# One scatter pass of a four-layer graph network: the attribute loads move to ScalarE's queue, a turn multiplies its own unit, and its sums are added in the last three steps

## The reference, cut to what matters

```python
def _gin_conv(x, src, dst, W_a, b_a, W_b, b_b):
    agg = jax.ops.segment_sum(x[src], dst, num_segments=N)
    h = agg + x
    ...
# in the spline layer, used much later:
v = edge_attr * (KS - 1)            # edge_attr: 3 numbers an edge
lo = jnp.floor(v); f = v - lo
...
basis = jnp.prod(w, axis=-1)        # weights of the 8 corners of a 4x4x4 grid cell
```

## Time and profile before

| | us |
|---|---|
| median of 3 runs | 14964.41 |
| the runs | 14935.78 to 14974.39 |
| span of the profiled execution | 14974.7 |
| TensorE's mean granted clock, share of full speed | 0.750 |
| start of the first basis of turn 0 (DVE) | 69.56 |
| start of the first basis of turn 12 (DVE) | 1876.23 |
| first product of the node phase behind the pass (PE) | 2054.82 |

### The profile page before, as it was taken

How to read it: one execution, slowest core, us unless ns; L and a number is a source line. 1 busy time by engine, 2 the same in 40 slices (tenths; PEclk the granted TensorE clock), 3 DMA queues, 4 the chain that set the end, 5 groups by cost and what they waited for, 6 DMA issues and landing times.

```text
span 14974.7 us, 218620 instructions
## 1 busy us (share of the span) xinstructions
PE 8996.9 (60%) x45542; PEld 5742.7 (38%) x45542; DVE 7299.2 (49%) x21322; ACT 1842.2 (12%) x1480; POOL 10378.6 (69%) x10674
## 2 busy tenths in 40 slices
PE   4655569986665665777776767776777760023225
PEld 2322223333443443444544444444445440023214
DVE  5555532323223224666666666666666661244446
ACT  4444420000000000111111111111111110000000
POOL 6666627775776775777775777775777765777772
PEclk7677669998787887777777877777777775566667
DMA  5666645554776774111111111111111111122221
GB/s 169 215 218 215 218 131 181 176 179 137 257 259 212 256 255 133 22 22 22 22 22 22 22 23 22 22 22 21 23 23 22 23 19 34 36 50 52 46 45 44
DMA packets 1184028, 1456.97 MB, mean 97 GB/s; under 512 B 415010, under 2 KB 627140, under 8 KB 1183173
## 3 DMA queue, kind: packets, MB, share of 16 engines
q10 hardware_dynamic: 565552, 1132.67, 21.6%
q0 software_dynamic: 338944, 197.81, 8.1%
q1 hardware_dynamic: 278678, 119.14, 3.5%
HBM read 1129.74 MB, written 319.05 MB: 97 GB/s over the span
## 4 chain that ended last, share of the span: by engine, by line
POOL 52%; issue 22%; PE 10%; DVE 6%; DMA 4%; DVEq 3%; ACT 1%; SPq 0%; POOLq 0%; ACTq 0%
POOL work L740 52%; PE ps L933 3%; PE ps L919 2%; PE ps L839 1%; DMA work<-tab_sp,idx 1%; DMA idx<-in_src_tile 1%; ACT nodes L1211 1%; PE ps L854 1%; DMA work<-in_x,idx 1%; DVE big L1709 1%; DVE work L1778 1%; DVEq L1635 1%; DVE work L1789 0%; PE ps L1036 0%; PE ps L953 0%
## 5 line engine op out<-in xcount | busy, mean ns | idle before, releaser
L740 POOL DMA_INDIRECT work<-tab_sp,idx x4992 | 4725.9, 947 | 1790.6 <-issue 1775.4
L933 PE MATMUL ps<-work 128*128 128x192 f32 x9984 | 2855.9, 418 | 1759.1 <-DVE work L1789 1035.7
L933 PEld LDWEIGHTS ps<-work 128*128 128x128 f32 x9984 | 1922.3, 229 | 2571.6 <-DVE work L1789 2244.1
L1789 DVE TENSOR_TENSOR work<-work,ps 128x192 f32 x4992 | 1762.6, 353 | 1628.8 <-PE ps L933 1101.0
L740 POOL DMA_INDIRECT work<-tab_att,idx x1664 | 1766.3, 1061 | 657.9 <-issue 507.0
L740 POOL DMA_INDIRECT work<-tab_gcn,idx x1664 | 1590.5, 956 | 556.5 <-issue 549.5
L854 PE MATMUL ps<-nodes,work 128*96 128x384 bf16 (+1 forms) x6664 | 1731.0, 381 | 174.5 <-DMA nodes<-counts_d 111.1
L919 PE MATMUL ps<-work,wk 128*32 128x144 f32 x10080 | 1780.3, 330 | 7.4 <-DVE work L1789 6.8
L740 POOL DMA_INDIRECT work<-in_x,idx x1248 | 1247.0, 999 | 702.5 <-issue 383.2
L1645 DVE TENSOR_TENSOR big<-big,ps 32x12 f32 (+2 forms) x3936 | 619.6, 157 | 2094.2 <-PE ps L827 1163.8
L1248 ACT ACTIVATE work<-zero 128x2496 f32<-128x2496 f32 x318 | 725.4, 2282 | 5489.0 <-PE ps L919 5482.9
(11 more groups left out here) (225 smaller groups left out, 5615.2 us busy)
## 6 DMA issues: line engine op xcount, KB each, us to landing
nodes<-counts_d ACTq DMA_DIRECT2D x468, 1056.0 KB
counts_d<-nodes ACTq DMA_DIRECT2D x104, 2376.0 KB
nodes<-counts_d ACTq DMA_DIRECT2D x144, 1320.0 KB
work<-counts_d ACTq DMA_DIRECT2D x117, 1056.0 KB
work<-tab_sp,idx POOLq DMA_INDIRECT x4992
work<-basis_d SPq DMA_DIRECT2D x312, 160.0 KB
work<-edge_rows SPq DMA_DIRECT2D x112, 320.0 KB
edge_rows<-work ACTq DMA_DIRECT2D x104, 320.0 KB, 2.4
```

Source lines behind the costliest of these rows:

```text
L740: pool.indirect_dma_start(out=rows(p, r)[:, t, 0:ROW[p]], out_offset=None, in_=TABLE[p], in_offset=bass.IndirectOffsetOnAxis(ap=idx[:, r, ...
L933: nc.tensor.matmul(ps[:, t % SUB, 0:K12 * TW], u0[:, s % 2, t % SUB, :], vb[:, t % SUB, :, :].rearrange("p k j -> p (k j)"), start=True, s ...
L1789: v.tensor_tensor(to, to, got, ALU.add).then_inc(mom_added.sem, 1)
```

## The change

SP keeps only the index loads. ACT asks for the attributes of steps 0 and 1 ahead of the pass, and for those of step k + 2 in step k. In ACT's queue the wait for the basis, and its write, move from ahead of the first eviction to behind the fifth. Turn i multiplies unit i instead of i - 1: two chunks in each of the first four steps, behind the third and the sixth tile of counts, and one in the fifth (turn 0, whose own counts must be written first, does three in each of its last three steps). The pieces are asked for behind the fourth and the seventh eviction of a step, the first two of a turn at the end of the turn before. DVE adds oct 0 in the sixth step of a turn, oct 1 in the seventh, octs 2 and 3 in the eighth (turn 0 adds all four at its end). Nothing is left to multiply after turn 12. The twelve register values of a step's near sums are read in one load instead of three of four.

```diff
+        def gin1_chunk(o, x, first):
+            c = 3 * (o - (STEPS - 3)) + x if first else 2 * o + x if x < 2 else NCH
+            return c if 0 <= c < NCH else None
+        def gin1_loads(o, b, first):
+            place = {(o, 3): [2 * o + 2], (o, 6): [2 * o + 3]}
+            if first:
+                place = {(4, 3): [0, 1], (5, 3): [2], (5, 6): [3], (6, 0): [4], (6, 3): [5], (6, 6): [6], (7, 0): [7],
+                         (7, 3): [8]}
+            return [c for c in place.get((o, b), []) if c < NCH]
...
 # SP, index_loads("gin1")
-                    def turn_(i, ahead):
-                        for o in range(STEPS):
-                            k, h = STEPS * i + o, o % 2
-                            if o < ahead:
-                                load_idx(i, o + ring)
-                            sp.wait_ge(bas_ready.sem, bas_ready.done(p, k - 2))
-                            sp.dma_start(attr[:, h, :, :].rearrange("p t d -> p (t d)"),
-                                         attr_tile[:, bass.ds(k * (G * 3), G * 3)]).then_inc(attr_in[h], 16)
...
                     with sp.Fori(0, turns - 1) as i:
-                        turn_(i, hpt)
-                    turn_(turns - 1, hpt - ring)
+                        for j in range(hpt):
+                            load_idx(i, j + ring)
+                    for j in range(hpt - ring):
+                        load_idx(turns - 1, j + ring)
...
 # PE, near_gin1
                             for b in range(3 * x, min(3 * x + 3, OCT)):
                                 build_counts(OCT * (STEPS * i + o) + b, b)
-                        if not first:
-                            dense(i - 1, o)
-                            if o == STEPS - 1:
-                                dense(i - 1, NCH - 1)
+                            c = gin1_chunk(o, x, first)
+                            if c is not None:
+                                dense(i, c)
...
-                for c in range(NCH):
-                    dense(NEAR_TURNS[p] - 1, c)
...
 # ACT, store_counts
+                def load_attributes(k, h):
+                    act.dma_start(attr[:, h, :, :].rearrange("p t d -> p (t d)"),
+                                  attr_tile[:, bass.ds(k * (G * 3), G * 3)]).then_inc(attr_in[h], 16)
...
-                        if not first:
-                            load_piece(i - 1, o + 1)
-                        act.wait_ge(bas_ready.sem, bas_ready.done("gin1", k))
-                        act.dma_start(basis_d[:, bass.ds(k * (G * BASIS), G * BASIS)],
-                                      bas[:, h, :, :].rearrange("p t k -> p (t k)")).then_inc(bas_out[h], 16)
                         for b in range(OCT):
...
+                            if b == 4:
+                                act.wait_ge(bas_ready.sem, bas_ready.done("gin1", k))
+                                act.dma_start(basis_d[:, bass.ds(k * (G * BASIS), G * BASIS)],
+                                              bas[:, h, :, :].rearrange("p t k -> p (t k)")).then_inc(bas_out[h], 16)
+                                if not (last and o >= STEPS - 2):
+                                    load_attributes(k + 2, h)
+                            for c in gin1_loads(o, b, first):
+                                load_piece(i, c)
...
-                    load_piece(i, 0)
-
+                    if not last:
+                        for c in range(2):
+                            load_piece(i + 1, c)
...
 # DVE, near_gin1
+                        firsts = firsts_from(SUBS * SUB * hpt * i + (3 * SUB * o + DENSE[p]), 3 * SUB)
                         for x, (j, s) in enumerate(gin1_subs(o)):
                             k = hpt * i + j
-                            add_near(p, k, s, firsts_from(k * G + (s * SUB + DENSE[p]), SUB))
+                            add_near(p, k, s, firsts[SUB * x:SUB * (x + 1)])
...
-                    if not first:
-                        add_dense(i - 1, SUB * (SUBS * hpt * i + SUBS * hpt))
+                        octs = {STEPS - 3: [0], STEPS - 2: [1], STEPS - 1: [2, 3]}.get(o, []) if not first else []
+                        if octs:
+                            add_octs(i, octs, SUB * (SUBS * hpt * i + 3 * (o + 1)))
+                    if first:
+                        add_octs(0, list(range(UNIT[p] // OCT)), SUB * SUBS * hpt)
...
-                add_dense(NEAR_TURNS[p] - 1, added.events(p))
```

More of the change, by code:

```diff
@@ L1209, in turn_ @@
                                 hold(act, "act", counts_out[h], 16 * (STEPS // 2) * i + 16 * (o // 2 + 1))
-                            out_ = staged_counts[:, h, :].rearrange("p (q m t w) -> p q m t w", q=3, t=OCT, w=LW)
                             nc.scalar.activation(out_[:, :, :, b, :],
@@ L1216, in turn_ @@
                                       staged_counts[:, h, :].rearrange("p (c n) -> p c n", c=NCH)).then_inc(counts_out[h], 16)
-                    load_piece(i, 0)
+                    if not last:
+                        for c in range(2):
+                            load_piece(i + 1, c)
+                for h in range(2):
+                    load_attributes(h, h)
                 turn_(0, first=True)
-                with act.Fori(1, NEAR_TURNS["gin1"]) as i:
+                with act.Fori(1, NEAR_TURNS["gin1"] - 1) as i:
                     turn_(i)
-                for c in range(1, NCH):
-                    load_piece(NEAR_TURNS["gin1"] - 1, c)
+                turn_(NEAR_TURNS["gin1"] - 1, last=True)
             def load_counts(p):
@@ L1663, in near_gin1, with add_octs @@
                 tl_base = turn_base[0]
-                def add_dense(unit, n_added):
+                def add_octs(unit, octs, n_added):
                     dve.wait_ge(added.sem, added.done(p, n_added - 1))
-                    add_unit(p, unit, [(SPLIT1, 7, 0)])
-                    dve.wait_ge(unit_added.sem, unit_added.done(p, adds[p] * (unit + 1) - 1))
+                    add_unit(p, unit, [(SPLIT1, 7, 0)], octs)
+                    dve.wait_ge(unit_added.sem, unit_added.done(p, adds[p] * unit + OCT * (octs[-1] + 1) - 1))
                 def turn_(i, tl, first=False):
```

3 lines of the change are left out of this document (2 added, 1 removed).

## The result

The changed kernel takes 14848.9 us (median of 4 runs, 14839.6 to 14862.78) against 14959.76 for the kernel before: a ratio of 0.9931, 95% interval 0.9917 to 0.9945. It is faster, by 111 us, but it lies above the predicted range of 14,600 to 14,800.

What follows compares the result with a forecast made beforehand. Consumers, held by attributes queued behind SP's waits for gathered rows, set the pace, not POOL. A turn: 150.0 - 16.3 - 4.5 - 8.0 + 8.0 = 129.2 us; the pass -297, so 14,667 us, range 14,600 to 14,800.

Steps and rivals of the forecast that it cites:

- Attributes in ACT's queue: ACT asks for attributes about two steps before use, so DVE's wait for them goes: -16.3 us a turn.
- late wait for the basis: ACT's basis wait moves behind the fifth eviction; DVE was not held by it, so priced at 0.
- The rule of the rings: A ring is consumed in order, so attributes in ACT's would stand behind up to 3592 KB, 10.5 us; term left at -16.3.
- The ninth chunk: Multiplied in the fifth step, so DVE no longer waits for it at the turn's end: -4.5 us a turn.
- the sums and the jump: The 15.6 us of adding and 3.2 us of jumping back at a turn's end stay, in other places: 0.
- The term of the transfers: A step with two pieces moves 4.76 MB, 13.6 us of all 16 engines, in three steps of eight: priced at 0.
- One register load for three: Ahead of DVE's near sums, one load saves 1.0 us a step: -8.0 a turn, with 0 and -11 as ends.
- The second chunk ahead of the third sub: In four steps PE's whole second chunk, 2.0 us, delays DVE's third near sums: +8.0 a turn, ends 0 and +19.6.
- Turn: One turn of the first pass falls from 150.0 to 129.2 us, still above POOL's 125.4.
- POOL never was the bound: Rival: POOL's gathers become the bound at 125.4 us a turn, 14,600 us in all; chance 0.13.
- The late attributes: Rival: attributes late again in ACT's ring or behind a waiting eviction, 16.3 comes back, 14,846 us; chance 0.04.
- PE at its lower clock: Rival: slower PE between the subs, +19.6 instead of +8.0 a turn, 14,818 us; chance 0.17 together with milder forms.

Runs made afterwards that it cites:

- kernel 1: Kernel before, with only ACT asking for the attributes and the basis wait behind the fifth eviction: 14732.02 us, ratio 0.9857.
- kernel 2: Changed kernel with three loads of four registers in a step in place of one of twelve: 14735.17 us, ratio 0.9861.
- experiment 4: Changed kernel with the next turn's first two pieces asked for in the sixth step, not at the turn's end: 14780.71 us, ratio 0.9891.
- experiment 6: experiment 4's kernel plus a useless 852 KB copy within device memory, asked for by ACT at each turn's end: 14822.86 us, ratio 0.9917.
- experiment 5: Changed kernel with a step's second chunk behind its last tile of counts and its piece asked for later: 14753.46 us, ratio 0.987.
- three loads with experiments 4 and 5: Changed kernel with three register loads, pieces asked for early and second chunk last, run only on slow chips: ratios 0.9927, 0.9935 and 0.9938 to the kernel before.
- 3, 4 and 5: Changed kernel with the one load at the step's start, pieces asked for early and second chunk last: 14689.07 us, ratio 0.9829.
- with 4 and 5: Changed kernel with pieces asked for early and second chunk last, on a slow chip: 20245.34 us with one load, 20199.48 with three.

## Why the prediction was wrong, step by step

*Attributes in ACT's queue, -16.3:* right. Alone, with the late wait for the basis, they gave 18.9. The 2.6 more come mainly from the idle time ahead of the third near sums, where DVE had waited for PE (7.0 us a turn before, 2.9 in kernel 1). The late wait for the basis, priced at 0, may have given them; the two were not run apart. The rule of the rings that spoke against it did not come to bear: in no full turn does DVE wait for attributes. It did once, at the first basis, 8.5 us behind ACT's other loads, which I had not counted.

*The ninth chunk, -4.5; the sums and the jump "stay, in other places: 0".* The first half came: the idle time ahead of the dense sums falls from 10.8 us a turn in kernel 1 to 5.7 in kernel 2. The second half is **one of the two steps that failed**. The sums kept their length, but the jump didn't: what the instruction queue fetches behind a jump comes by the same 16 DMA engines, and before the change almost nothing else was on them at that moment. I had read that share and used it for the clock alone. The pieces moved to the end of the turn made it +5.5 a turn (experiment 4), and experiment 6 brought the delay back with other bytes. The term of the transfers had left out just these pieces: it counts two in each of three steps, and the first two of a turn, asked for right behind the eighth step's counts write, come on top.

*One register load for three, -8.0, with 0 and -11 as ends:* **the step that failed most**. It was +7.5, outside both ends, as experiment 2 shows by undoing this part alone: +10.5 ahead of the near sums, some of it given back at the end of the turn. Three things were wrong in it. A load costs by the register, not by the load: of the durations in the earlier trace rows, 339 ns is a load of four and 598 ns is one of eight for the dense sums, with nothing slowed down in either; I could have told them apart in the trace by what follows them. The long ones have a cause, the counts write in flight, and the one load stands where that write nearly always is (70 of 79). And small loads lie partly under queued one-hots; a big one ahead of the first sub lies under a basis product of 0.42 us only. A saving of nothing was among its bounds, but a loss should have been too; no reason excluded it. The Trainium skill, "DMA: Bandwidth & Descriptors", section "Latency and other measured facts", has a register load at about 600 ns at the least. The 339 ns in the earlier trace rows already disagree, and a price by the load, which that floor suggests, is what the runs refute.

*The second chunk ahead of the third sub, +8.0:* right in place and size in the changed kernel, 7.5 (experiment 5), and the sign that was named for it, a wait near 2 us ahead of the third sub in the first four steps, is there (2.0 to 2.3). With three loads it looks cheaper: from kernel 1 to kernel 2 the third gap grows by 3.9 us a turn and the second shrinks by 3.9.

*Turn:* 150.0 - 18.9 (experiment 1) = 131.1; the own unit in five steps and its sums, with three loads, +5.4 = 136.5 (experiment 2); the one load +7.5 = 144.0. That this closes proves nothing, since each part is the distance between two kernels of one chain. The forecast had -16.3, +3.5 and -8.0. Of the 14.8 us missing, 15.5 are the load. The middle term, +3.5 against +5.4, came out close by luck: by the table the end of a turn costs +9.4 there (3.3 to 12.7), the dense sums' idle time is -5.1, and the near sums' is +0.3, where the forecast had 0, -4.5 and +8.0.

*The pass around the turns:* turn 0 and the end were right within 10 us.

*Rivals:* POOL never was the bound; its wait for PE shrank to 220.7 only. The late attributes had the time almost to the microsecond (14,846), with a cause that the trace doesn't show in any full turn. PE at its lower clock (14,818) asked for 4.9 us at the third sub in each of four steps; by experiment 5 it was 1.9 (7.5 / 4).

*What stays open:* whether three loads with experiments 4 and 5 reach about 125 us a turn on a chip like the first ones, where the sum of the parts and POOL's floor of 125.4 meet. It never ran on one, and as three loads make the end of a turn longer the parts needn't add up. The fastest version measured there is the one with 3, 4 and 5 (14689.07 us, 160 less than the changed kernel; the changed kernel ran on another chip, and by the ratios it is 0.9829 against 0.9931). Why the load costs less with 4 and 5 on the late chips than in kernel 1 is open in part. Some of it is at the end of a turn: with 4 and 5 that is 9.4 us with three loads and 7.8 with one, in kernel 1 it is 3.3 and 4.1, which makes 2.4 of the 4.6 us between the two prices. What makes those chips slow is open too.

## What to carry to other kernels

In these runs a load of registers is priced by its registers and by whether a large write is in flight where it stands; before several are gathered into one, see which of them lie under queued work, since only the uncovered part can be saved. A jump back on a full engine is a small DMA fetch on the critical path: keep large transfers from being asked for just ahead of it, and look at it again after every edit of the loop, since the edit of experiment 2 made it 2.8 us longer. When a change has several parts, price each by both signs and time them apart; here one part alone was better than the whole.

## What was not expected of the hardware

- The time from DVE's branch to its next instruction goes with the traffic on the DMA engines: 2.7 to 3.0 us when they are nearly idle, 3.4 to 4.1 with the rest of a counts write, 6.1 to 6.9 with 852 KB more, 6.4 to 7.3 with two pieces of 1056 KB. One to three packets of 8 KB start on the instruction queue in that time. With the same pieces and three loads in a step it is 7.5 to 7.8 and four packets.
- A register load of 4, 8 or 12 takes 0.35, 0.60 or 0.85 us, and 1.08, 1.59 or 2.43 in the 9 us behind the request for a write of 2376 KB; other traffic that fills the engines leaves a load of 4 at 0.35.
- Three chips took 20,320 to 20,540 us for a kernel that took 14,940 to 14,960 on others. In the first pass DVE's and ACT's operations last as long there, the DMA share is 0.48 instead of 0.73 and PE's granted clock 0.64 instead of 0.76; the cause isn't shown.
